# One list of 39 expert groups, built in three stages, in place of two lists of 31 and 15

## The reference

```python
gate_scores = softmax(x @ Wg + bg)                    # 8 experts
top_probs = softmax(top_k(gate_scores, 2))            # two experts for each row
out = sum over the two of  top_prob * (relu(x @ W1[e] + b1[e]) @ W2[e] + b2[e])    # 128 -> 512 -> 128
```

## Time and profile before

| what | value |
|---|---|
| time, median of 3 runs | 883.94 us (882.31 to 884.08) |
| span of the profiled execution | 889.5 us |
| PE busy | 721.8 us (81%) |
| DVE busy | 715.8 us (80%) |
| POOL busy | 639.2 us (72%) |
| ACT busy | 531.9 us (60%) |
| DMA | 148.91 MB, mean 167 GB/s |

### The profile page before, as it was taken

How to read it: one execution, slowest core, us unless ns; L and a number is a source line. 1 busy time by engine, 2 the same in 40 slices (tenths; PEclk the granted TensorE clock), 3 DMA queues, 4 the chain that set the end, 5 groups by cost and what they waited for, 6 DMA issues and landing times. The chain is left out here.

```text
span 889.5 us, 12694 instructions
## 1 busy us (share of the span) xinstructions
PE 721.8 (81%) x3977; PEld 491.0 (55%) x3977; DVE 715.8 (80%) x1060; ACT 531.9 (60%) x1272; POOL 639.2 (72%) x481
## 2 busy tenths in 40 slices
PE   6577578888888889888878888847888998899992
PEld 3343344554445455455535545524565787799982
DVE  4789999999999999999999999999435245455782
ACT  4777569669768877876976795681243342233230
POOL 1278899678989889889998988997422445645552
PEclk9788779999999999899999999987899999999997
DMA  4545575274464646347425533960643346675952
GB/s 99 192 149 146 182 266 192 82 251 145 158 178 155 192 121 203 122 135 211 157 109 184 172 120 107 280 203 25 190 129 105 109 158 196 223 253 168 368 183 76
DMA packets 83917, 148.91 MB, mean 167 GB/s; under 512 B 11201, under 2 KB 56143, under 8 KB 83850
## 3 DMA queue, kind: packets, MB, share of 16 engines
q1 hardware_dynamic: 78858, 139.55, 49.3%
q0 software_dynamic: 4992, 8.54, 2.8%
HBM read 115.34 MB, written 39.27 MB: 174 GB/s over the span
## 5 line engine op out<-in xcount | busy, mean ns | idle before, releaser
L1451 POOL TENSOR_TENSOR prod<-hst,BC 128x1024 f32<-128x1024 f32 x128 | 301.4, 2362 | 62.7 <-DVE hst L1663 49.6
L1663 DVE TENSOR_TENSOR_SCAN hst<-dA,Rp 128x1024 f32<-128x1024 f32 x128 | 292.2, 2283 | 6.4
L1188 ACT ACTIVATE dA<-dtm,Aneg 128x255 f32<-128x255 f32 x512 | 214.8, 496 | 66.0 <-DVE hst L1663 64.1
L1571 POOL DMA_INDIRECT y2d<-prod,back x92 | 91.7, 997 | 125.5 <-DVE prod L1964 103.8
L1456 POOL TENSOR_TENSOR prod<-prod 128x512 f32<-128x512 f32 x128 | 163.6, 1288 | 2.4
L1654 DVE TENSOR_TENSOR Rp<-BC,Rp 128x1024 f32<-128x1024 f32 x128 | 157.0, 1226 | 7.8 <-DMA BC<-bcd 0.6
L638 PE MATMUL Y<-prod,ident 128*128 128x256 f32 x512 | 139.2, 405 | 22.8 <-POOL prod L1456 18.0
L638 PEld LDWEIGHTS Y<-prod,ident 128*128 128x128 f32 x512 | 99.1, 201 | 57.9 <-POOL prod L1456 22.5
L638 PE MATMUL Mb<-hpad,winT 128*128 128x512 f32 (+1 forms) x176 | 82.5, 617 | 15.1 <-ACT xh L1137 13.6
L638 PEld LDWEIGHTS Rp<-BC,xh 128*128 128x128 f32 x736 | 89.1, 192 | 4.8 <-issue 2.6
L638 PE MATMUL Rp<-BC,xh 128*128 128x128 f32 x736 | 89.9, 275 | 0.6 <-DVE prod L1964 0.6
(11 more groups left out here) (254 smaller groups left out, 1215.9 us busy)
## 6 DMA issues: line engine op xcount, KB each, us to landing
BC<-bcd SPq DMA_DIRECT2D x63, 1024.0 KB, 5.4
BC<-recs SPq DMA_DIRECT2D x46, 578.0 KB
xsd<-blank SPq DMA_DIRECT2D x18, 1056.0 KB, 12.4
dtm<-xsd SPq DMA_DIRECT2D x46, 132.0 KB
recs<-in_L_ffn_W SPq DMA_DIRECT2D x16, 256.0 KB
xin<-in_x SPq DMA_DIRECT2D x8, 256.0 KB, 5.8
x2d<-x2o SPq DMA_DIRECT2D x8, 256.0 KB, 5.6
E<-x2d SPq DMA_DIRECT2D x4, 512.0 KB
```

What stands on the lines that cost most here:

```text
L1188: m = A(dA[:, k % RING, i, 1:SEQ], dtm[:, r % 2, d, b * SEQ + 1:(b + 1) * SEQ], ACT.Exp, scale=Aneg[:, d, c * NC + i:c * NC + i + 1])
L1451: TT(prod[:, k % RING, :, :], hst[:, k % RING, :, :], BC[:, (k // 2) % BCR, 1, :, :], ALU.mult).then_inc(s_pd, 1)
L1571: pool.indirect_dma_start(out=y2d[:, :], out_offset=bass.IndirectOffsetOnAxis(ap=at, axis=0), in_=yr[:, j % YR, i, :], in_offset=None, bou ...
L1663: v.tensor_tensor_scan(hst[:, k % RING].rearrange("p n s -> p (n s)"), dA[:, k % RING].rearrange("p n s -> p (n s)"), U.rearrange("p n s - ...
```

## The change

There is one region of 4096 rows for each expert and one list of 39 = 32 + 7 groups. The table is made in three stages, since the list starts before rounds 6 and 7 are routed: entries 0 to 16 from the counts after six rounds, 17 to 20 after seven, 21 to 38 after eight (`STAGES`). The first stages take only groups that are full by then, whatever the counts are, and `taken` notes how far each expert has got. Table 0 is made where it was, table 1 in step 5, table 2 in step 13. SP waits before entry 17 for table 1 and the scatters of round 6, before entry 21 for table 2 and those of round 7. The scatters of round 7 go out two in a step (steps 13 to 16) in place of one (13 to 20). The results of pieces 0 to 2 are loaded in one go before the loads of group 38; `results` of pieces 0 and 1 are in steps 34 to 37, those of pieces 2, 3 and 4 behind the last group.

```diff
-PARTS = [Part(0, SPLIT, 0, 0)]
-PARTS.append(Part(SPLIT, ROUNDS, EXPERTS * PARTS[0].region + SPARE, PARTS[0].groups))
-GROUPS = PARTS[0].groups + PARTS[1].groups
+GROUPS = 2 * ROWS // GROUP + EXPERTS - 1
+def full_groups(rounds):
+    return -(-(2 * rounds * TOK - EXPERTS * (GROUP - 1)) // GROUP)
+STAGES = ((0, full_groups(SPLIT), SPLIT), (full_groups(SPLIT), full_groups(SPLIT + 1), SPLIT + 1), (full_groups(SPLIT + 1), GROUPS, ROUNDS))
+SOME = tuple(2 * r * TOK // GROUP + EXPERTS - 1 for r in (SPLIT, SPLIT + 1, ROUNDS))
+MOST = ROWS // GROUP
-FINAL_AT = PARTS[1].group + 5
+FINAL_AT = SOME[0] + 3
...
-            for j in range(RINGS, PARTS[1].group):
+            for j in range(RINGS, GROUPS):
+                for i in (1, 2):
+                    if j == STAGES[i][0]:
+                        sp.wait_ge(s_tab, i + 1)
+                        sp.wait_ge(s_xs, 16 * 2 * NTT * STAGES[i][2])
+                if j == GROUPS - 1:
+                    scattered(SOME[0])
+                    for i in range(3):
+                        for c in range(2):
+                            load_results(i, c)
                 load_rows(j)
                 load_weights(j)
...
+            scattered(SOME[1])
+            for c in range(2):
+                load_results(3, c)
+            for i in range(2):
                 store_out(i)
             scattered(GROUPS)
+            for c in range(2):
+                load_results(4, c)
+            for i in range(2, len(PIECES)):
                 store_out(i)
...
-                    if j == group_of(ROUNDS + 1, STEPS - 2) + n:
+                    if j == group_of(ROUNDS + 1, STEPS - 2) + n // 2:
                         scatter(ROUNDS - 1, n)
...
+            def whole_groups(to, over, started):
+                test, least = (ALU.is_gt, 0) if started else (ALU.is_ge, 1)
+                each = [P, EXPERTS, MOST]
+                then(v.tensor_tensor(over, full[:, :].unsqueeze(2).to_broadcast(each),
+                                     rows[:, least:least + MOST].unsqueeze(1).to_broadcast(each), test))
+                then(v.tensor_reduce(to, over, AX.X, ALU.add))
+                then(v.tensor_scalar(to, to, float(GROUP), None, ALU.mult))
+            def entries(i, parts, pa, pasts_):
...
+                then(v.tensor_tensor(pa, numbers.unsqueeze(2).to_broadcast(wide), ends[:, 0:q].unsqueeze(1).to_broadcast(wide), ALU.is_ge))
+                then(v.tensor_tensor(pasts_, pa, jump[:, 0:q].unsqueeze(1).to_broadcast(wide), ALU.mult))
+                then(v.tensor_reduce(start[:, at], pasts_, AX.X, ALU.add))
...
+            def taken(i, parts):
...
+                then(v.memset(cut[:, 0:1], float(lo * GROUP)))
+                then(v.tensor_scalar(cut[:, 1:q + 1], ends[:, 0:q], float(hi * GROUP), None, ALU.min))
+                then(v.tensor_tensor(count[:, 0:q], cut[:, 1:q + 1], cut[:, 0:q], ALU.subtract))
+                for a in range(parts):
+                    then(v.tensor_tensor(bounds[:, 0, :], bounds[:, 0, :], count[:, a * EXPERTS:(a + 1) * EXPERTS], ALU.add))
...
                 lasts(drain, a, b + 1)
+                if j == group_of(ROUNDS, 12) + 1:
+                    group_table(1)
                 if j == group_of(ROUNDS + 1, 12) + 1:
-                    group_table(1)
+                    group_table(2)
-                if FINAL_AT <= j < FINAL_AT + 2 * (SPLIT * FINAL // ROUNDS):
+                if FINAL_AT <= j < FINAL_AT + 4:
                     results(*divmod(j - FINAL_AT, 2))
             tile_out(GROUPS - 1)
-            for i in range(SPLIT * FINAL // ROUNDS, len(PIECES)):
+            for i in range(2, len(PIECES)):
                 for c in range(2):
                     results(i, c)
```

More of the change, by code:

```diff
@@ L608, in _ @@
                     store_x2(ROUNDS - 2)
-                if j == 3 * RINGS - 3:
+                if j == 2 * RINGS + 3:
                     store_x2(ROUNDS - 1)
[L611 to L624, removed]
+                if 0 <= j - 2 * RINGS - 4 < FINAL:
+                    load_residual(j - 2 * RINGS - 4)
+            scattered(SOME[1])
+            for c in range(2):
+                load_results(3, c)
+            for i in range(2):
                 store_out(i)
             scattered(GROUPS)
[L627 to L630, removed]
+            for c in range(2):
+                load_results(4, c)
+            for i in range(2, len(PIECES)):
                 store_out(i)
@@ L1428, in _ @@
                 lasts(drain, a, b + 1)
[L1429 removed]
+                if j == SOME[0] - 2:
                     act.wait_ge(s_wt, 2)
@@ L1899, in _, with then @@
             tabled_in = [Rp[:, k, :, :].rearrange("p n s -> p (n s)") for k in range(2)]
[L1901 to L1921 removed]
+            def then(ins):
+                tabled[0] += 1
+                ins.then_inc(s_t, 1)
+                v.wait_ge(s_t, tabled[0])
@@ L1922, in group_table @@
+            def group_table(i):
+                over = crowds[min(i, 1)]
                 if i == 0:
                     v.wait_ge(s_sc, ROUNDS * STEPS)
-                then(v.tensor_tensor(full, base[:, (part.last - 1) % 2, :], first[:, i, :], ALU.subtract))
-                then(v.tensor_tensor(over, full.unsqueeze(2).to_broadcast(each), rows[:, 0:most].unsqueeze(1).to_broadcast(each), ALU.is_gt))
-                then(v.tensor_reduce(full, over, AX.X, ALU.add))
-                then(v.tensor_scalar(full, full, float(GROUP), None, ALU.mult))
@@ L1934, in group_table @@
-                then(v.tensor_reduce(expert[:, at], pa, AX.X, ALU.add))
-                then(v.tensor_scalar(table[:, 1, at], expert[:, at], float(EXPERTS - 1), None, ALU.min))
-                v.sem_inc(s_tab, 1)
+                then(v.tensor_tensor(full[:, :], base[:, (STAGES[i][2] - 1) % 2, :], first[:, :], ALU.subtract))
+                if i == 0:
+                    lo, hi, _ = STAGES[0]
+                    wide = [P, hi, EXPERTS]
+                    held, hops, closes = goal[:, 0, :], jump[:, 0:EXPERTS], ends[:, 0:EXPERTS]
+                    pa, ps_ = (tabled_in[k][:, P:P + hi * EXPERTS].rearrange("p (g e) -> p g e", e=EXPERTS) for k in range(2))
+                    whole_groups(held, over, False)
+                    then(v.tensor_scalar(hops, held, -1.0, float(ROWS), ALU.mult, ALU.add))
+                    then(v.tensor_tensor_scan(closes, onesb[:, 0:EXPERTS], held, 0.0, ALU.mult, ALU.add))
+                    then(v.tensor_tensor(pa, rows[:, 0:hi].unsqueeze(2).to_broadcast(wide), closes.unsqueeze(1).to_broadcast(wide), ALU.is_ge))
+                    then(v.tensor_tensor(ps_, pa, hops.unsqueeze(1).to_broadcast(wide), ALU.mult))
+                    then(v.tensor_reduce(tabled_in[0][:, 0:hi], ps_, AX.X, ALU.add))
+                    then(v.tensor_tensor(table[:, 0, 0:hi], tabled_in[0][:, 0:hi], rows[:, 0:hi], ALU.add))
+                    then(v.tensor_reduce(expert[:, 0:hi], pa, AX.X, ALU.add))
+                    then(v.tensor_copy(table[:, 1, 0:hi], expert[:, 0:hi]))
+                    v.sem_inc(s_tab, 1)
+                    whole_groups(goal[:, 2, :], over, True)
+                    taken(0, 1)
+                    return
@@ new lines, in group_table @@
+                if i == 1:
+                    whole_groups(goal[:, 1, :], over, False)
+                whole_groups(goal[:, 2 + i, :], over, True)
+                aims = (0, 1) if i == 1 else (2, 3, 4)
+                for a, k in enumerate(aims):
+                    then(v.tensor_tensor(bounds[:, a + 1, :], bounds[:, a, :], goal[:, k, :], ALU.max))
+                then(v.tensor_tensor(count[:, 0:len(aims) * EXPERTS].rearrange("p (a e) -> p a e", e=EXPERTS), bounds[:, 1:len(aims) + 1, :],
+                                     bounds[:, 0:len(aims), :], ALU.subtract))
@@ L1938, in tile_norm @@
+                entries(i, len(aims), past[:, :], pasts[:, :])
+                if i == 1:
+                    taken(1, 2)
             def tile_norm(j):
```

115 lines of the change are left out of this document (56 added, 59 removed).

## The result

The changed kernel takes 875.38 us (median of 4 runs, 872.83 to 879.13), the kernel before beside it 883.12 (880.61 to 884.08): ratio 0.9891, 95% interval [0.9853, 0.9929]. The prediction was 864.7, range 857 to 872.

The account below looks back on a forecast made before the run. The prediction took PE, busy 81% of the span, as the bound. Its terms, -26.5 + 3.4 + 3.5 + 0 - 2.1 + 2.5 = -19.2 us, took 883.94 to 864.7 us, range 857 to 872.

Parts of the forecast that it names:

- Seven groups fewer: From `tile_out(22)` to the last one: 39 list entries, not 46, so seven plain groups go; -26.5 us.
- Table 1: Step 5: chain of 30 operations, 7.1 us, 3.7 us spare, the rest stops PE; +3.4 us, bounds 2 to 7.1.
- Table 2: Step 13: 23 operations, 6.8 us, replace 12 of 3.35 us, nothing covers the rest; +3.5 us, bounds 2.5 and 5.
- The clock: PE's waits in steps 6 and 14: a half-speed stretch for one of the two; +2.5 us, bounds 0 and 6.4.
- Table 0, "0 us": Before `tile_norm(0)`: table 0.4 us shorter, seven extra operations covered by DVE's wait for rows; 0 us, 1.7 without cover.
- The end, -2.1: Behind the last `tile_out`: 6.5 us of results fit DVE's 7.92 us wait, eight fewer instructions afterwards; -2.1 us.
- "Hidden otherwise": Work counted at no cost, such as SP's hold before entry 21 for round 7's scatters, with 7 us for rows.
- The rival on the slow groups: Groups 14 to 22: with round 7's scatters earlier, four or five may run at 3.80; -4 us, 861 us; chance 0.14.
- the rival with the long slow clock: Both table waits bring the long slow clock, chains at their upper bounds; +8 us, 873 us; chance 0.07.
- loads collide: Six result loads at once: DVE waits for piece 0, entry 21 or group 38 late; +5 us, 870 us; chance 0.14.

Follow-up runs that it names:

- the repeats: The kernel before and the changed kernel, each run again unchanged for a second trace: 883.53 us and 874.23 us.
- spread1: Changed kernel with table 1's operations made in three pieces, in steps 6, 7 and 9: 872.41 us, ratio 0.9858.
- the five edits: Changed kernel with table 0 in PSUM, a wait for the last scatter, tables 1 and 2 in pieces, round 7's scatters earlier: 856.43 us, ratio 0.9695.

## Why the prediction was wrong

- **Seven groups fewer**, -26.5: right. From `tile_out(22)` to the last one the repeats differ by 27.4 us, and seven groups put back cost 27 in the trace.
- **Table 1**, +3.4: right, 3.3 in the trace, and `spread1` shows it to be the overhang beyond DVE's slack.
- **Table 2**, +3.5: right, 3.6 for group 13.
- **The clock**, +2.5: right for the two waits that it named, with one slow stretch and not two. It followed the 5.01 us wait (0.63 over group 14, 2.2 us) and in this trace not the 3.13 us wait. Of the eight traces with table 1 in one piece, three have a slow group 6 too (9.61 to 9.69 us, not 8.04). So the prediction's reading of the Trainium skill, TensorE: Matmul & The Clock Gate, "Part 1: The HAM clock gate", by which both waits bring a slow stretch, came true in three of eight. A third wait was not foreseen, that for `tile_norm(1)` behind the late table 0; what its slow stretch costs stands under that term.
- **Table 0, "0 us"**: failed. The step compared numbers of elements and reckoned with cover in DVE's wait for rows. But that wait is on the path: rows can't be loaded before the table is made, and SP's first load came some 4 us later behind the last scan. Its seven extra operations were hidden as said. What was late were small operations moved from PSUM to SBUF, which wait out whatever is left of POOL's running product. The earlier trace rows show an operation with PSUM operands at 0.42 us; the term assumed that operations in SBUF go at such a pace there too. Against the 31.96 us of the repeat of the kernel before, the loss to `tile_out(0)` was 2.1 us in three of the eight traces with table 0 as changed (33.6 to 34.1) and 4.8 in five (36.5 to 36.8), where the granted clock fell to 0.50 at or behind PE's wait of 2.9 to 4.0 us for `tile_norm(1)`. The first trace of the kernel before has 34.1 as well, with a longer slow stretch at the end of its mixer, so a single pair of traces could have hidden the 2.1.
- **The end, -2.1**: failed, with the sign turned; it was +1.75 between the repeats and +2.45 between the first traces. The arithmetic held: 6.5 us of DVE work, 6.4 in the trace, in a wait of 7.92. What failed was the assumption that DVE's work leaves the wait as it is: the wait ends with the loads behind POOL's last scatter, and DVE's work made that scatter five times as long.
- **"Hidden otherwise", entry 21, "7 us to come"**: failed. It took 4.73 us for a group, from a stretch that was slow in that one execution. At 3.8 us three groups are 11.4 us, not 14, and POOL, at 5.2 us a step, falls behind by 1.4 in each. Of the 7 us, 3.2 were left: the last scatter was through on POOL at 774.77, and DVE wanted the rows at 777.93. Scatter's landing and load took 4.4 us from there, to 779.15; SP had issued the load only at 776.91. The term had no price for these two. Cost: 2.9 us in groups 18 and 19. The rival on the slow groups said that the gate "gets tight"; no price followed.
- **The trace of before** ended 5.6 us above the median and took 8.0 us more for groups 14 to 22 than the repeat, 5.9 of them with PE idle. Nothing was to be recovered there.
- **The bounds** were added up too tightly. The bounds that the terms carry reach from about 859 to 876 us in sum (3.7 + 1.5 + 2.1 + 3.9 above 864.7), not from 861 to 869, and the range stopped at 872. In the rival with the long slow clock, 3.9 for the clock and 5.2 for the chains make 9.1, not 8, so 874.

Sum of what the runs showed: -27.4 + 3.3 + 3.6 + 2.2 + 2.9 + 4.8 + 1.75 = -8.9 us, against 9.3 for the repeats and 7.7 in the first comparison.
This takes the repeats' 4.8 for table 0, clock included; entry 21 is the mean of both traces. That the sum comes near is no proof of each part, the five edits are.
The rival nearest to the outcome in time was both waits with a long slow clock (873), but its mechanism is not what happened; "loads collide" had the late entry 21 in it, for another reason. The results' loads did not hold anyone.

## What to carry to other kernels

A producer in front of a gate is on the path however idle its own engine is: before hiding work in a wait, ask what ends the wait and whether the work touches that. When steps get faster, recompute every fixed distance that was counted in steps, above all the load that waits for a queue of another engine. And take one more trace before building on a stretch that looks slow without a named cause.

## What the runs showed of the hardware

DVE and POOL get in each other's way at SBUF, in both directions, and it depends on where DVE's operands lie. Beside POOL's products, DVE's operations on 8 to 136 elements with all inputs in SBUF ended with the running product (0.79 to 2.28 us for 0.17 to 0.3); with one input in PSUM they ran through. In the other direction, DVE's back-to-back additions with two SBUF inputs stretched the issue of an indirect DMA on POOL from 0.98 to 4.95 us. They did so to the last scatter only. The one before it, wholly beside the same run of 24 additions, took 1.13 us, as did those beside the eight additions of steps 34 to 37; why, no run shows.

The Trainium skill, SBUF — State Buffer, "SBUF: two separate sides", says that whichever engine starts first holds the shared pair of ports for its whole instruction and the other blocks; of DVE's operations it names those in a two-port mode and those with two SBUF inputs. For the first direction the traces agree: operations on 8 and 17 elements ended 0.03 to 0.04 us behind the product, those on 128 and 136 elements 0.15 to 0.16. The same section tells of descriptors starved on GpSimd beside VectorE's two-port operations; here additions with two SBUF inputs did it, at the 4.95 us above.

Behind PE's wait of 5.0 us group 14 was slow (5.48 to 6.61 us) in every one of the eight traces with table 2 in one piece. Behind the wait of 3.14 us at group 6 the clock fell in three of eight traces, with 1.6 us between them, and two of these three run the same instructions up to there as the changed kernel, whose own traces have no slow stretch there. Exactly those five traces that had a slow stretch ahead of `tile_out(0)` had none at group 6. What decides between the two isn't shown.
